# Attention with a rotary cache and a LoRA layer on one core: the query projection moved ahead of the third scores, the value products behind them, weight pieces taken three steps ahead

## The chip, the core and the metric

One core of one Trainium2 chip runs the whole program. The metric is the device time in microseconds (us) of one execution. TensorE (PE in the profile, with PEld for its weight loads), VectorE (DVE), ScalarE (ACT), GpSimd (POOL) and the queue of SyncE (SP) each work through their own list of instructions in order; one waits for another by semaphores.

## The reference

Two residual layers follow each other, x of 8 batches x 128 tokens x 512 features, all in float32:

```
q, k, v = x Wq^T (32 heads of 128), x Wk^T, x Wv^T (8 heads of 128 each)
q, k    = rope(rmsnorm(q) * wq), rope(rmsnorm(k) * wk)
keys    = [512 keys of the paged cache (masked from cache_seqlens on), 128 new keys]; values likewise
o       = softmax(q keys^T / sqrt(128) + mask) values, 4 query heads to a key head
x       = x + o Wo^T
x       = x + x W^T + 2 * sum_e gate[e] * (x A[e]^T) B[e]^T, gates from the top two of 8 experts
```

## The kernel before

The attention is cut into 64 groups, `g` = 0 to 63: eight key heads, the outer part, times eight batches. A group has four query heads (h = 0 to 3), 640 keys and 128 tokens. Every product on TensorE is made of float32r operands in three passes, `hi*hi + hi*lo + lo*hi`. So every operand is split into two tiles: ScalarE copies it to the high one (`..._hi`), and VectorE subtracts that from the original and writes the low one (`..._lo`, helper `low`, line 743).

The loop runs over steps `s` = 0 to 64, and each engine has its own `step(s)`, written out by hand; the order in that code is the order on the engine. The work of three groups is mixed in a step. With short names that the rest of this document uses, TensorE does in step s, before the change:

- S0, S1: scores of heads 0 and 1 of group s (`scores(h)`, line 1196), 6 products each, into `ps_s`
- V: value products of group s-1 (lines 289 to 291, out<-in `ps_w<-pt_..,v_..`), 15 products of 512 columns
- S2, then T0: scores of head 2; four transposes of the probabilities of head 0 (line 1205)
- Q: query projection of group s+2 (`project_queries`, `ps_w<-w_..,xt_..`), 12 products of 512 columns
- S3, T1, then Y: the output projection of group s-1 (`ps_w<-wo_..,o_..`), 12 products
- T2, QT and KTC (transposes of rotated queries and cached keys of group s+1), the key and value projection of group s+2 with KTN (new keys turned) in it, T3, and TN (line 1273), which ends the step

A head h of group s goes S, then on VectorE `rowmax(h)` (line 833, which adds the mask and takes the maximum), on ScalarE `exps(h)` (line 599), on VectorE the reciprocal `over_sum(h)` (line 840), on ScalarE `norm(h)` (line 605), then T. The value products end in `o_hi` (ScalarE) and then `o_lo` (VectorE), and Y waits for `o_lo` (`d_olo`).

The queries of group s+1 are normed and rotated in step s. ScalarE squares them, VectorE sums the squares (`sumsq`, line 799), GpSimd makes `meansq` (439), `rstd` (441, a power of five numbers) and `wr` (459), VectorE multiplies `u<-raw,wr` (879). Then two products of `u` start: `m<-u,sin` on VectorE (806, called m2 in the code) and `rot<-u,cos` on GpSimd (447), and GpSimd adds the two (465).

`ps_w` has four banks of PSUM, given out by rotation over the list `UNITS`; `wait_bank` makes TensorE wait until the unit that had the bank before was read. The weights of the next key head come in eight pieces (`W_AT` for q, k, v, `WO_AT` for Wo: step to pieces; `W_MID`, `WO_MID`: a second place in early steps). ScalarE splits a piece's high half in the step that the table names, VectorE its low half (`w_lo`, `wo_lo`) in the next, and the SP queue loads it in the step before. Steps 0 to 8 also hold work that is done once: masks, splits of x, the first Wo.

## Time and profile before

| what | value |
|---|---|
| time, median of 3 runs | 1173.83 us (1172.22 to 1174.01) |
| the profiled execution | 1173.76 us, span of its instructions 1172.0 us |
| TensorE busy | 1147.9 us, 98% |
| VectorE, ScalarE, GpSimd busy | 920.5, 934.3, 764.8 us |
| TensorE's mean granted clock | 0.998 of full speed |

The span reaches from the first to the last instruction. TensorE's products overlap, so their durations add up to more than the time between their starts; below, lengths on TensorE are differences of starts.

### The profile page before, as it was taken

The page shows a single profiled execution, that of the slowest core. Times are in us where ns is not written, and L with a number is a line of the kernel's source. Part 1 is how long each engine was busy: PE and PEld are TensorE (multiplying, and loading weights), DVE is VectorE, ACT ScalarE, POOL GpSimd, SP SyncE. Part 2 cuts the span into 40 slices and gives each one's busy share as a digit, 9 for nine tenths or more (in the row PEclk, how much of TensorE's full clock was granted, in tenths as well). Part 3 has the DMA queues.
Part 4 walks back from the last instruction along what each step waited for, and adds up shares of the span by engine and source line. Part 5 has one row for each costly group of instructions (what it writes and reads, how often), then busy time and mean ns, then how long its engine had stood idle before and what let it go on. Part 6 is the DMA issues. An engine that isn't in the chain of part 4 may idle for free.

```text
span 1172.0 us, 20839 instructions
## 1 busy us (share of the span) xinstructions
PE 1147.9 (98%) x6932; PEld 1025.8 (88%) x6932; DVE 920.5 (79%) x1885; ACT 934.3 (80%) x1832; POOL 764.8 (65%) x834
## 2 busy tenths in 40 slices
PE   6899999999999999999999999999999999999898
PEld 5788888889989988988998899899889989989787
DVE  7878788777887877788787778878777887877746
ACT  6788887888888888888888888888888888888741
POOL 4767666767666766776676676667667666766500
PEclk9999999999999999999999999999999999999999
DMA  6333332122123212312321221222122122211001
GB/s 242 130 96 108 105 100 89 54 95 95 61 83 96 89 54 95 95 53 90 95 87 57 95 95 56 88 95 86 58 95 95 52 89 93 83 48 61 19 1 72
DMA packets 53738, 98.11 MB, mean 84 GB/s; under 512 B 8704, under 2 KB 25984, under 8 KB 53376
## 3 DMA queue, kind: packets, MB, share of 16 engines
q1 hardware_dynamic: 41344, 63.21, 15.6%
q0 software_dynamic: 12288, 33.57, 9.5%
q8 instruction: 57, 0.93, 0.3%
q14 instruction: 49, 0.40, 0.1%
HBM read 90.45 MB, written 6.29 MB: 83 GB/s over the span
## 4 chain that ended last, share of the span: by engine, by line
PE 92%; DVE 3%; ACT 2%; issue 1%; DVEq 0%; ACTq 0%
PE ps_s L1196 18%; PE ps_w L289 18%; PE ps_w L291 18%; PE ps_w L290 18%; PE ps_w L1205 9%; PE ps_w L1273 3%; PE ps_w L1172 2%; PE ps_w L1179 2%; PE ps_s L1127 2%; DVE pt_lo L743 1%; ACT ps L599 1%; DVE ps L833 1%; PE ps_w L1150 1%; ACT ps L605 1%; DVE wo_lo L743 0%
## 5 line engine op out<-in xcount | busy, mean ns | idle before, releaser
L429 POOL DMA_INDIRECT kv_raw<-kv,rows x256 | 255.0, 996 | 97.0 <-issue 62.3
L599 ACT ACTIVATE ps<-ps,negmax 128x640 f32<-128x640 f32 x256 | 211.8, 827 | 91.0 <-DVE negmax L833 91.0
L605 ACT ACTIVATE ps<-ps,recip 128x640 f32<-128x640 f32 x256 | 213.0, 832 | 67.3 <-DVE recip L840 67.3
L743 DVE TENSOR_TENSOR pt_lo<-ps_w,pt_hi 128x512 fp32r<-128x512 f32 x322 | 209.9, 683 | 67.7 <-ACT pt_hi L610 66.5
L833 DVE CUSTOM_DVE_ANT_0 ps<-ps_s,mask 128x640 f32<-128x640 f32 x256 | 204.0, 815 | 2.2 <-PE ps_s L1196 1.2
L289 PE MATMUL ps_w<-w_hi,xt_hi 128*128 128x512 f32 (+1 forms) x496 | 182.5, 368 | 3.6 <-DVE w_lo L743 2.2
L610 ACT ACTIVATE pt_hi<-ps_w 128x512 fp32r<-128x512 f32 x256 | 151.8, 593 | 24.3 <-PE ps_w L1205 21.3
L447 POOL TENSOR_TENSOR rot<-u,cos 128x640 f32<-128x640 f32 x63 | 99.4, 1578 | 107.0 <-DVE u L879 107.0
L291 PE MATMUL ps_w<-w_hi,xt_lo 128*128 128x512 f32 (+1 forms) x496 | 167.4, 338 | 0.0
L290 PE MATMUL ps_w<-w_lo,xt_hi 128*128 128x512 f32 (+1 forms) x496 | 167.0, 337 | 0.0
L1205 PE MATMUL ps_w<-cst,ps 128*128 128x128 f32 x1024 | 154.1, 273 | 4.6 <-DVE pt_lo L743 2.2
L465 POOL TENSOR_TENSOR rot<-rot,m 128x320 f32<-128x320 f32 x126 | 108.7, 885 | 51.6 <-DVE m L806 51.5
L1205 PEld LDWEIGHTS ps_w<-cst,ps 128*128 128x128 f32 x1024 | 123.8, 141 | 16.0 <-issue 5.7
L290 PE MATMUL ps_w<-pt_lo,v_hi 128*128 128x512 f32 x320 | 125.4, 392 | 0.0
L289 PE MATMUL ps_w<-pt_hi,v_hi 128*128 128x512 f32 x320 | 125.3, 392 | 0.0
L1196 PE MATMUL ps_s<-kt_hi,qt_hi 128*128 128x320 f32 x512 | 122.2, 320 | 3.1 <-DVE kt_lo L743 2.8
L291 PE MATMUL ps_w<-pt_hi,v_lo 128*128 128x512 f32 x320 | 124.9, 390 | 0.0
L806 DVE TENSOR_TENSOR m<-u,sin 128x640 f32<-128x640 f32 x64 | 123.2, 1925 | 0.0
L1196 PE MATMUL ps_s<-kt_hi,qt_lo 128*128 128x320 f32 x512 | 117.4, 311 | 0.0
L840 DVE RECIPROCAL recip<-rowsum 128x1 f32<-128x1 f32 x256 | 41.0, 160 | 97.3 <-ACT ps L599 96.9
L1196 PE MATMUL ps_s<-kt_lo,qt_hi 128*128 128x320 f32 x512 | 117.1, 310 | 0.0
L289 PE MATMUL ps_w<-wo_hi,o_hi 128*128 128x512 f32 x256 | 105.6, 412 | 0.0
(172 smaller groups left out, 2642.1 us busy)
## 6 DMA issues: line engine op xcount, KB each, us to landing
xt_hi<-xsplit SPq DMA_DIRECT2D x56, 256.0 KB, 3.1
xt_lo<-xsplit SPq DMA_DIRECT2D x56, 256.0 KB, 3.7
w_raw<-wqkv SPq DMA_DIRECT2D x56, 192.0 KB, 3.8
wo_raw<-wo SPq DMA_DIRECT2D x56, 128.0 KB, 4.1
kv_raw<-kv,rows POOLq DMA_INDIRECT x256, 3.9
y<-x SPq DMA_DIRECT2D x8, 256.0 KB, 3.8
out<-y SPq DMA_DIRECT2D x8, 256.0 KB, 2.3
xsplit<-xt_hi SPq DMA_DIRECT2D x6, 256.0 KB, 3.3
```

What stands on the lines that cost most here:

```text
L289: nc.tensor.matmul(out_ap, a_hi, b_hi, start=start and k == 0, stop=False)
L290: nc.tensor.matmul(out_ap, a_hi, b_lo, start=False, stop=False)
L291: last = nc.tensor.matmul(out_ap, a_lo, b_hi, start=False, stop=stop and k == n - 1)
L429: pool.indirect_dma_start(kv_raw[:, g % 2, t, :], None, kv[:, :], bass.IndirectOffsetOnAxis(rows[:, g % B, t:t + 1], 0)).then_inc(s_kv[g % ...
L599: nc.scalar.activation(ps[:, h, :], ps[:, h, :], ACT.Exp, bias=negmax[:, s % 2, h:h + 1], scale=-1.0, accum_out=rowsum[:, s % 2, h:h + 1]) ...
L605: nc.scalar.activation(ps[:, h, :], ps[:, h, :], ACT.Copy, scale=recip[:, s % 2, h:h + 1]).then_inc(a_norm, 1)
L610: nc.scalar.activation(pt_hi[:, 0:CT, h, :], bank(f"T{h}").rearrange("p (t q) -> p t q", t=CT), ACT.Copy).then_inc(a_pt, 1)
L743: return nc.vector.tensor_tensor(out_ap, full, hi.bitcast(F32), ALU.subtract)
L806: nc.vector.tensor_tensor(m2[:], u[:], sin[:, g % B, :].unsqueeze(1).to_broadcast([P, NH, D]), ALU.mult).then_inc(d_m2, 1)
L833: nc.vector.tensor_tensor_reduce(out=halves(ps[:, h, :]), in0=ps_s[:, h % 2, :, 0:KH], in1=halves(mask[:, b, :]), scale=-SCALE, scalar=3.0 ...
L1196: last = nc.tensor.matmul(ps_s[:, h % 2, half, 0:KH], a, c[:, half * KH:(half + 1) * KH], start=n == 0, stop=n == 2)
L1205: last = nc.tensor.transpose(bank(f"T{h}")[:, t * S:(t + 1) * S], ps[:, h, t * P:(t + 1) * P], ident)
```

## The change

The order on three engines moves. On TensorE, Q stands behind S1 now, then S2, V and T0. On ScalarE the copy of the queries and exps(2), norm(2) stand ahead of `o_hi`. On VectorE the first piece of weights is taken behind the sum of squares instead of behind over_sum(1), and `o_lo` behind `m` instead of ahead of rowmax(2). The bank list is turned by one place to match. The tables `W_MID` and `WO_MID` are gone; pieces are split one step earlier. Masks, splits of x and the first Wo move to other places of steps 0 to 5. No instruction is added or removed in the steady steps.

```diff
@@ -68,7 +68,7 @@
...
-UNITS = ["O", "T0", "Q", "T1", "Y", "T2", "QT", "KTC", "KV", "KTN", "T3", "TN"]
+UNITS = ["Q", "O", "T0", "T1", "Y", "T2", "QT", "KTC", "KV", "KTN", "T3", "TN"]
 NU = len(UNITS)
@@ -79,12 +79,10 @@
...
 OP = REP * HID // B
-W_AT = {2: [2], 3: [4], 4: [6], 5: [7]}
-W_MID = {1: 0, 2: 1, 3: 3, 4: 5}
+W_AT = {1: [0, 1], 2: [2, 3], 3: [4, 5], 4: [6, 7]}
 for n in range(B, HK * B):
-    W_AT[n - 2] = [n]
-WO_AT = {3: [0], 4: [1], 5: [2], 6: [4], 7: [6], 8: [7]}
-WO_MID = {6: 3, 7: 5}
+    W_AT[n - 3] = [n]
+WO_AT = {5: [0, 1], 6: [2, 3], 7: [4, 5], 8: [6, 7]}
 for n in range(B, (HK - 1) * B + 2):
@@ -252,6 +250,12 @@
...
             return ps_w[:, UNITS.index(unit) % NBANK, :]
+
+        def query_bank(g):
+            return bank("T0") if g == 1 else bank("Q")
+
+        def keys_values_bank(g):
+            return bank("O") if g == 0 else bank("KV")
@@ -390,16 +394,12 @@
...
                     x_transposed(2, 1, 0, 4)
-                if s + 1 in W_MID:
-                    w_load(W_MID[s + 1])
                 for n in W_AT.get(s + 1, ()):
...
                     natural_x(1)
-                if s + 1 in WO_MID:
-                    wo_load(WO_MID[s + 1])
                 for n in WO_AT.get(s + 1, ()):
@@ -559,12 +559,12 @@
...
                 wait(act, d_u, g - 2)
-                nc.scalar.activation(raw[:, g % 2, 0:QW], bank("Q"), ACT.Copy).then_inc(a_q, 1)
+                nc.scalar.activation(raw[:, g % 2, 0:QW], query_bank(g), ACT.Copy).then_inc(a_q, 1)
...
                 wait(act, p_v, g - 2, 2)
-                nc.scalar.activation(raw[:, g % 2, QW:WW], bank("KV")[:, 0:2 * D], ACT.Copy).then_inc(a_kv, 1)
+                nc.scalar.activation(raw[:, g % 2, QW:WW], keys_values_bank(g)[:, 0:2 * D], ACT.Copy).then_inc(a_kv, 1)
@@ -617,6 +617,8 @@
...
                         first_wo_split(h)
+                if HB < s + 3 < B:
+                    split_x(s + 3)
                 if has(s):
@@ -624,6 +626,12 @@
...
                     expert_products(0)
+                if has(g2):
+                    queries(g2)
+                turn_x(s, "Q")
+                if has(s):
+                    exps(2)
+                    norm(2)
                 if has(s - 1):
@@ -641,25 +649,17 @@
...
                     nc.scalar.activation(v_hi[:, CT, :], raw[:, s % 2, QW + D:WW], ACT.Copy).then_inc(a_vhi, 1)
-                    if HB <= s + 3 < B:
-                        split_x(s + 3)
-                    exps(2)
-                    norm(2)
-                if has(g2):
-                    queries(g2)
-                turn_x(s, "Q")
                 if has(s):
                     probs(1)
-                    if s in W_MID:
-                        w_split(W_MID[s])
-                    if s in WO_MID:
-                        wo_split(WO_MID[s])
                     exps(3)
                     norm(3)
-                    probs(2)
                 if s == 0:
...
                         first_wo_split(h)
+                elif s == 1:
+                    split_x(HB)
+                if has(s):
+                    probs(2)
                 if has(g1):
@@ -850,18 +850,37 @@
...
                     sums_of_squares(g1)
+                if s == 0:
+                    split_x(3)
+                elif s == 1:
+                    first_wo_split(2)
+                for n in W_AT.get(s - 1, ())[:1]:
+                    w_split(n)
+                for n in WO_AT.get(s - 1, ())[:1]:
+                    wo_split(n)
                 if has(s):
...
                     add_base(0)
-                if s in (1, 2):
-                    masks(3 * s - 1, 3 * s + 1)
-                for n in W_AT.get(s - 1, ()):
+                if s == 1:
+                    first_wo_split(3)
+                for n in W_AT.get(s - 1, ())[1:]:
                     w_split(n)
-                for n in WO_AT.get(s - 1, ()):
+                for n in WO_AT.get(s - 1, ())[1:]:
                     wo_split(n)
+                if has(s):
+                    rowmax(2)
+                if has(g1):
+                    wait(dve, p_wr, g1 - 1)
+                    wait(dve, d_ss, g1)
+                    nc.vector.tensor_tensor(u[:].rearrange("p h d -> p (h d)"), raw[:, g1 % 2, 0:QW + D],
+                                            wr[:].rearrange("p h d -> p (h d)"), ALU.mult).then_inc(d_u, 1)
+                if has(s):
+                    over_sum(2)
+                if has(g1):
+                    times_sine(g1)
                 if has(s - 1):
@@ -870,53 +889,35 @@
...
                 if has(s):
-                    rowmax(2)
-                if s == 0:
-                    split_x(3)
-                if has(g1):
-                    wait(dve, p_wr, g1 - 1)
-                    wait(dve, d_ss, g1)
-                    nc.vector.tensor_tensor(u[:].rearrange("p h d -> p (h d)"), raw[:, g1 % 2, 0:QW + D],
-                                            wr[:].rearrange("p h d -> p (h d)"), ALU.mult).then_inc(d_u, 1)
-                if has(s):
-                    over_sum(2)
-                if has(g1):
-                    times_sine(g1)
-                if has(s):
                     rowmax(3)
...
                     over_sum(3)
+                if HB <= s + 3 < B:
+                    split_x(s + 3)
+                elif s == 0:
+                    first_wo_split(0)
+                if 0 <= s < HB + 1:
+                    masks(s + 2, s + 3)
                 if 0 < s <= B:
...
                     nc.vector.tensor_tensor(yb, bank("Y"), yb, ALU.add).then_inc(d_y, 1)
-                if HB <= s + 3 < B:
-                    split_x(s + 3)
-                if s == 0:
-                    first_wo_split(0)
-                    first_wo_split(1)
                 if has(s):
                     probs(2)
-                if s == 0:
-                    first_wo_split(2)
                 if has(g1):
...
                 if s == 0:
-                    first_wo_split(3)
-                if s in W_MID:
-                    w_split(W_MID[s])
-                if s in WO_MID:
-                    wo_split(WO_MID[s])
+                    first_wo_split(1)
                 if has(g1):
                     new_keys(g1)
-                if s in (1, 2):
-                    masks(3 * s + 1, 3 * s + 2)
+                if s == HB:
+                    masks(B - 1, B)
                 for unit in ("QT", "KTC", "KV", "KTN"):
@@ -1135,22 +1136,29 @@
...
                         pe.wait_ge(d_wlo, SPLITS + g)
-                wait_bank(pe, g - 2, "Q")
+                if g >= 2:
+                    wait_bank(pe, g - 2, "Q")
...
                 wh, wl = head_weights(g // B)
-                three_passes(bank("Q"), [(xt_tile(0, g, k), xt_tile(1, g, k), wh[:, k, 0:QW], wl[:, k, 0:QW])
+                three_passes(query_bank(g), [(xt_tile(0, g, k), xt_tile(1, g, k), wh[:, k, 0:QW], wl[:, k, 0:QW])
                                          for k in range(KC)], before=weights_split).then_inc(pe_q, 1)
...
             def turn_new_keys(g):
-                wait_bank(pe, g - 1, "KTN")
+                if g == 0:
+                    wait(pe, a_kv, 0)
+                else:
+                    wait_bank(pe, g - 1, "KTN")
                 nc.tensor.transpose(bank("KTN")[:, 0:S], rot[:, REP, :], ident).then_inc(pe_ktn, 1)
...
             def project_keys_values(g, new_keys_of=None):
-                wait_bank(pe, g - 2, "KV")
+                if g == 1:
+                    wait(pe, a_q, 0)
+                elif g >= 2:
+                    wait_bank(pe, g - 2, "KV")
@@ -1159,15 +1167,17 @@
...
                 wh, wl = head_weights(g // B)
-                three_passes(bank("KV")[:, 0:2 * D], [(xt_tile(0, g, k), xt_tile(1, g, k), wh[:, k, QW:WW], wl[:, k, QW:WW])
+                three_passes(keys_values_bank(g)[:, 0:2 * D], [(xt_tile(0, g, k), xt_tile(1, g, k), wh[:, k, QW:WW], wl[:, k, QW:WW])
                                                       for k in range(KC)], before=between).then_inc(pe_kv, 1)
...
                     pe.wait_ge(d_scaled, NH - 2)
-                wait(pe, p_rot, g - 1, 2)
-                wait_bank(pe, g - 1, "QT")
+                    wait(pe, a_q, 1)
+                else:
+                    wait(pe, p_rot, g - 1, 2)
+                    wait_bank(pe, g - 1, "QT")
                 for h in range(REP):
@@ -1210,29 +1220,25 @@
...
                     second_layer(0)
+                if has(g2):
+                    project_queries(g2)
+                turn_x(s, "Q")
+                if has(s):
+                    scores(2)
                 if has(s - 1):
-                    wait(pe, d_pt, s - 1, 5, CT)
+                    wait(pe, d_pt, s - 1, 5)
                     wait(pe, p_v, s - 1, 2)
                     wait_bank(pe, s, "O")
-
-                    def new_keys_split(t):
-                        if t == CT:
-                            wait(pe, d_pt, s - 1, 5)
-
                     three_passes(bank("O"), [(v_hi[:, t, :], v_lo[:, t, :],
                                               pt_hi[:, t, :, :].rearrange("p h q -> p (h q)"),
-                                              pt_lo[:, t, :, :].rearrange("p h q -> p (h q)")) for t in range(KT)],
-                                 before=new_keys_split).then_inc(pe_o, 1)
+                                              pt_lo[:, t, :, :].rearrange("p h q -> p (h q)")) for t in range(KT)]
+                                 ).then_inc(pe_o, 1)
                 if s == G:
...
                 if has(s):
-                    scores(2)
                     turn_probs(0)
-                if has(g2):
-                    project_queries(g2)
-                turn_x(s, "Q")
                 if has(s):
...
                     turn_probs(1)
```

TensorE, the stretch that ends with the first product of Y, a steady step, before (first row: last product of Q; L1196 is S3, L1205 is T1):

```order
L291 MATMUL ps_w<-w_hi,xt_lo 128x512
L1196 MATMUL ps_s<-kt_hi,qt_hi 128x320 x2
L1196 MATMUL ps_s<-kt_lo,qt_hi 128x320 x2
L1196 MATMUL ps_s<-kt_hi,qt_lo 128x320 x2
L1205 MATMUL ps_w<-cst,ps 128x128 x4
L289 MATMUL ps_w<-wo_hi,o_hi 128x512
```

The same stretch of the change (first row: last product of V; then T0, S3, T1):

```order
L295 MATMUL ps_w<-pt_hi,v_lo 128x512
L1215 MATMUL ps_w<-cst,ps 128x128 x4
L1206 MATMUL ps_s<-kt_hi,qt_hi 128x320 x2
L1206 MATMUL ps_s<-kt_lo,qt_hi 128x320 x2
L1206 MATMUL ps_s<-kt_hi,qt_lo 128x320 x2
L1215 MATMUL ps_w<-cst,ps 128x128 x4
L293 MATMUL ps_w<-wo_hi,o_hi 128x512
```

The last value product now stands two transposes and one head's scores ahead of Y; before, Q and S2 stood between as well.

VectorE in the same step, from over_sum(0) to `m`, before (RECIPROCAL is over_sum, ISA the two halves of rowmax):

```order
L840 RECIPROCAL recip<-rowsum 128x1
L799 TENSOR_REDUCE sumsq<-u 128x5
L840 RECIPROCAL recip<-rowsum 128x1
L743 TENSOR_TENSOR w_lo<-w_raw,w_hi 128x384
L743 TENSOR_TENSOR wo_lo<-wo_raw,wo_hi 128x256
L743 TENSOR_TENSOR o_lo<-ps_w,o_hi 128x512
L833 ISA ps,negmax<-ps_s,mask 128x640
L833 ISA negmax 128x1
L879 TENSOR_TENSOR u<-raw,wr 128x640
L840 RECIPROCAL recip<-rowsum 128x1
L806 TENSOR_TENSOR m<-u,sin 128x640
```

And in the change, to `o_lo`:

```order
L840 RECIPROCAL recip<-rowsum 128x1
L799 TENSOR_REDUCE sumsq<-u 128x5
L743 TENSOR_TENSOR w_lo<-w_raw,w_hi 128x384
L743 TENSOR_TENSOR wo_lo<-wo_raw,wo_hi 128x256
L840 RECIPROCAL recip<-rowsum 128x1
L833 ISA ps,negmax<-ps_s,mask 128x640
L833 ISA negmax 128x1
L878 TENSOR_TENSOR u<-raw,wr 128x640
L840 RECIPROCAL recip<-rowsum 128x1
L806 TENSOR_TENSOR m<-u,sin 128x640
L743 TENSOR_TENSOR o_lo<-ps_w,o_hi 128x512
```

The low halves of the weights moved ahead of over_sum(1), and `o_lo` moved behind five rows, the long `m` among them.

ScalarE in the same step, from the second exps to `o_hi`, in the change (L599 exps, L605 norm, L562 the copy of the queries); before, `o_hi` stood right behind the first norm here:

```order
L599 ACTIVATE ps,rowsum<-ps,negmax 128x640
L605 ACTIVATE ps<-ps,recip 128x640
L562 ACTIVATE raw<-ps_w 128x512
L599 ACTIVATE ps,rowsum<-ps,negmax 128x640
L605 ACTIVATE ps<-ps,recip 128x640
L638 ACTIVATE o_hi<-ps_w 128x512
```

So `o_hi` now waits, by its place in the queue, for norm(2), and norm(2) for the third reciprocal on VectorE, which stands behind `u`.

## Rows read from the trace of the kernel before

**Rows 1.** Windows view, all engines: length; busy and (instructions) by engine; clock; DMA

```profile
41.00:60.00 19.00, 18.96 (x104) 16.95 (x104) 13.81 (x30) 13.93 (x28) 13.02 (x14) 0.91 0.41 143
590.00:607.00 17.00, 17.00 (x105) 15.34 (x104) 13.53 (x27) 14.13 (x29) 12.10 (x14) 1.00 0.25 82
```

**Rows 2.** Chain that ended last, S0 with S1 of a step: start, us, what

```profile
41.04 3.48 PE ps_s L1196 x12
...
113.78 2.00 PE ps_s L1196 x12
...
218.20 1.75 PE ps_s L1196 x12
...
1073.49 1.76 PE ps_s L1196 x12
```

**Rows 3.** Timeline of TensorE, one steady step: start, us, instruction

```profile
611.48 0.54 PE L1196 MATMUL ps_s<-kt_hi,qt_hi 128*128 128x320 f32 x2
...
620.82 0.45 PE L1196 MATMUL ps_s<-kt_hi,qt_hi 128*128 128x320 f32 x2
...
622.05 0.48 PE L289 MATMUL ps_w<-wo_hi,o_hi 128*128 128x512 f32 x1
```

**Rows 4.** Timeline of VectorE, the same step

```profile
614.97 0.82 DVE L799 TENSOR_REDUCE sumsq<-u 128x5 f32<-128x640 f32 x1
...
616.84 0.54 DVE L743 TENSOR_TENSOR w_lo<-w_raw,w_hi 128x384 fp32r<-128x384 f32 x1
617.30 0.42 DVE L743 TENSOR_TENSOR wo_lo<-wo_raw,wo_hi 128x256 fp32r<-128x256 f32 x1
618.31 0.69 DVE L743 TENSOR_TENSOR o_lo<-ps_w,o_hi 128x512 fp32r<-128x512 f32 x1 [0.59 <-ACT o_hi L630]
...
619.65 0.82 DVE L879 TENSOR_TENSOR u<-raw,wr 128x640 f32<-128x640 f32 x1
...
620.81 1.99 DVE L806 TENSOR_TENSOR m<-u,sin 128x640 f32<-128x640 f32 x1
```

**Rows 5.** Timeline of ScalarE, the same step

```profile
616.96 0.83 ACT L605 ACTIVATE ps<-ps,recip 128x640 f32<-128x640 f32 x1 [0.23 <-DVE recip L840]
617.70 0.57 ACT L630 ACTIVATE o_hi<-ps_w 128x512 fp32r<-128x512 f32 x1
```

**Rows 6.** Timeline of GpSimd, the same step

```profile
615.88 0.20 POOL L439 TENSOR_SCALAR meansq<-sumsq 128x5 f32<-128x5 f32 x1 [0.95 <-DVE sumsq L799]
...
617.45 1.39 POOL L459 TENSOR_TENSOR wr<-nw,rstd 128x640 f32<-128x640 f32 x1
```

**Rows 7.** Timeline of all engines, ahead of the first step

```profile
17.86 0.82 DVE L806 TENSOR_TENSOR m<-u,sin 128x640 f32<-128x640 f32 x1
...
18.11 0.62 POOL L439 TENSOR_SCALAR meansq<-sumsq 128x5 f32<-128x5 f32 x1 [2.77 <-DVE sumsq L799]
...
18.59 0.82 DVE L992 TENSOR_TENSOR rot<-u,cos 128x640 f32<-128x640 f32 x1
...
18.82 1.66 POOL L441 TENSOR_TENSOR rstd<-meansq,mhalf 128x5 f32<-128x5 f32 x1
```

**Rows 8.** Timeline of all engines, step 0: the pair of `m` and `rot`

```profile
29.45 1.26 POOL L459 TENSOR_TENSOR wr<-nw,rstd 128x640 f32<-128x640 f32 x1
...
31.18 0.81 DVE L879 TENSOR_TENSOR u<-raw,wr 128x640 f32<-128x640 f32 x1
...
31.91 0.15 DVE L840 RECIPROCAL recip<-rowsum 128x1 f32<-128x1 f32 x1
32.02 0.82 DVE L806 TENSOR_TENSOR m<-u,sin 128x640 f32<-128x640 f32 x1
...
32.07 2.22 POOL L447 TENSOR_TENSOR rot<-u,cos 128x640 f32<-128x640 f32 x1 [1.36 <-DVE u L879]
```

**Rows 9.** The same view, step 0: T0 behind the norm that releases it

```profile
27.04 0.83 ACT L605 ACTIVATE ps<-ps,recip 128x640 f32<-128x640 f32 x1 [0.23 <-DVE recip L840]
...
27.92 0.66 PE L1205 MATMUL ps_w<-cst,ps 128*128 128x128 f32 x4 [0.86 <-ACT ps L605]
```

14 lines of the change are left out of this document (7 added, 7 removed).

## The prediction

> **What bounds the kernel now.** I read the windows view first. In a steady stretch of 17 us TensorE is busy for all of it, VectorE and ScalarE for about 14 us each [rows 1]. So TensorE is the bound, and a change can only give back what TensorE idles, or add to it. Next the chain of waits, which shows where each step begins (S0 and S1 stand as one piece of 12 products). From 218.20 to 1073.49 lie 50 steps: 17.106 us each [rows 2]. The early steps are longer. Steps 1 to 4 take 113.78 - 41.04 = 72.74 us, 4.32 above four steady ones; steps 5 to 10 take 104.42, 1.78 above six steady ones [rows 2]. Of the 4.32, S0 and S1 of step 1 account for 3.48 - 1.75 = 1.73 us [rows 2]: there the granted clock fell, to a mean of 0.91 over 19 us against 1.00 later [rows 1]. By the two levels, 1.2 and 2.4 GHz, that is about 3.4 us at the lower one, after a step 0 in which TensorE often stood still. What is left, 2.6 us in steps 1 to 4, is TensorE waiting at the step's start for VectorE.
>
> The rest of the argument is one steady step, the one that starts at 611.48, and I count from there. Y starts at 10.57 [rows 3]. In the trace o_lo is done at 618.31 + 0.69, which is 7.52 [rows 4], so Y has 3 us to spare. `u` starts at 8.17 and `m` at 9.33.
>
> **What costs nothing.** The steady step holds the same products in another order. Between V and Y now stand T0, S3 and T1. S3 with T1 takes 622.05 - 620.82 = 1.23 us [rows 3], T0 at most 0.44 (estimated from T1's part of it), so V ends at about 8.9 and its last result leaves the array near 9.1. Y stays at 10.57 if nothing holds it. Q at the place of V needs the bank that V needed before, so it waits for the same copy. V waits for all of its operands at once now, but starts later by Q and S2. Moving weight pieces one step earlier puts their loads one step earlier in SP's queue, ahead of the x loads that stand behind them; each of those has a step or more before its use, so I take nothing. The cover is a whole step; without it each late load would stop Q.
>
> **The new chain to Y.** It has three parts.
>
> First, the way to `u`. The sum of squares starts at 3.49 and VectorE is free for the next instruction after about 0.73 us, as `m` and the next product show [rows 7]. There now stands `w_lo`: 4.22 to 4.76. `wo_lo` follows after 617.30 - 616.84 = 0.46 and lasts 0.42 [rows 4]: 4.68 to 5.10. GpSimd starts `meansq` at 4.40, where it took 0.20 [rows 6]. Ahead of step 0 the trace shows what happens when VectorE works on two SBUF tiles then: `meansq` took 0.62 and ended at 18.73, 0.05 after `m` ended, although the next VectorE product had begun at 18.59; the `rstd` behind it started 0.09 later, took 1.66 and ended at 20.48, 1.07 after that second product [rows 7]. So GpSimd is held while such an instruction runs, and gets in between two of them. Applied here: `meansq` ends at 4.81, `rstd` at 5.10 + 1.07 = 6.17, `wr` starts 0.09 later, 6.26. `wr` took 1.39 behind a `wo_lo` that still ran as it began [rows 4, 6]; nothing does now, and without that it takes 1.26 [rows 8]. It ends at 7.52, and with 0.05 for the handover (T0 started at 27.92, the norm ended at 27.87 [rows 9]) `u` runs from 7.57 to 8.39. In the trace it starts at 8.17.
>
> Second, `m`. It takes 1.99 in the steady step [rows 4], but 0.82 in step 0 [rows 8]. In step 0 the reciprocal was ready, `m` started 0.84 after `u` and GpSimd's `rot` 0.89 after it; `m` ran through and `rot` took 2.22 [rows 8]. In the steady step the reciprocal comes late, `rot` goes first and `m` is held until `rot` is done. In the new order exps(2) stands ahead of V's copy. Norm(1) starts at 5.48 [rows 5], the copy of the queries 0.74 later, exps(2) some 0.5 behind that and takes about 0.9 with its sum, estimated from the norm's 0.83: it ends near 7.65, well before `u` does. So the case of step 0 comes in every step: `m` from 8.41 to 9.23. VectorE gets back 1.17 us a step, which by itself is worth nothing on the path.
>
> Third, the copies. The third reciprocal starts at 7.57 + 0.73 = 8.30 and lasts 0.15 [rows 8]; with 0.05 for the handover norm(2) starts on ScalarE at 8.50. `o_hi` follows a norm after 617.70 - 616.96 = 0.74 [rows 5]: 9.24, later than V's end. `o_lo` follows after 618.31 - 617.70 = 0.61 [rows 4, 5]: 9.85, and lasts 0.69: 10.54. With 0.05 to reach TensorE Y starts at 10.59, 0.02 later than it would, or a little more if the weight load ahead of its first product has to be waited for too. Each of these seven handovers is good to 0.01 or 0.02, so the bounds are nothing and 0.13 a step. I choose 0.08, above the walk, because an early result gives nothing back while each late one adds its delay. Behind Y on TensorE are T2, the turned queries and keys, and T3, and ScalarE and VectorE follow them, so the wait lengthens each step and is not caught up. There are 61 such steps (1 to 61): 4.9 us.
>
> The Trainium skill bears on the first part. "SBUF — State Buffer", section "Who interferes with whom", says that a VectorE instruction with two SBUF inputs and a GpSimd instruction that reads SBUF exclude each other for a whole instruction; the trace agrees with its 0.62 for 0.20 [rows 7]. The same page, in its section on the bandwidth-pool intuition, states a release about 115 ns after VectorE ends where the row shows 0.05. By the page `meansq` would end 0.065 later, and 61 steps differ by 4 us. The sum goes by the row.
>
> **What is given back.** In steps 2 to 4 low halves of weights stood ahead of the new keys on VectorE, and S0 of the next step waits for those. They are gone from there. In their place ScalarE now has two high pieces ahead of its new-key copy in steps 1 to 4. A piece is of the size of `w_lo`, 0.54 [rows 4], and most of it fits into the time in which ScalarE waits for the new keys; I take 0.15 us a step (bounds 0 and 0.54). So of 2.6 us 2.0 come back (bounds 0.4 and 2.6). The 1.78 us of steps 5 to 10 I did not break down; the change has fewer pieces in their middle, and I take 0.4 (bounds 0 and 1.78). In step 0 Q runs while TensorE waited for norm(0), 0.86 us [rows 9]; the step ends on VectorE's and GpSimd's work, and I take 0.6 (bounds 0 and 1.2). Together 3.0. The last two steps have no Q; Y comes later there, and `m` is shorter: nothing, within 0.7 either way.
>
> **Sum.** 1173.76 of the profiled execution, less 3.0, plus 4.9: 1175.7. The median, 1173.83, is the same within 0.1.
>
> **The rivals.**
> - A, the forecast: a wait of 0.03 to 0.13 at Y. The sum reaches from 1172.0 to 1179.5. Chance 0.60.
> - B, no wait at Y: GpSimd isn't held by `w_lo`, `u` starts at about 7.3 and `o_lo` is done by 10.4. For it: in the steady trace `w_lo` runs at 616.84, between `meansq` at 615.88 and `wr` at 617.45, and did not stretch that distance of 1.57 visibly [rows 4, 6]. Against it: rows 7. Only the 3.0 us remain: 1169.5 to 1171.5. Chance 0.15.
> - C, ends on the slow side by far: `rot` keeps its lead over `m`. The lead that decides is 0.05 us, in one pair of rows [rows 8]. If the reciprocal or the wait on `u` makes `m` start more than 0.05 later, `m` ends 622.80 - 619.65 = 3.15 after `u` starts, as in the trace [rows 4]: 10.72, `o_lo` at 11.33, Y at 11.4. That is 0.82 x 61 = 50 us, less 3.0: 1221. Against it: the same start in step 0, with the reciprocal ready. Chance 0.07.
> - D, a larger wait of the same kind, 0.15 to 0.4 a step: `meansq` has to wait for `wo_lo` as well, since that one is queued before `w_lo` ends (then `u` starts 0.28 later). Rows 7 speak against it. 9 to 24 us less 3.0: 1180 to 1195. Chance 0.14.
> - E, 0.04: step 0 leaves TensorE busy enough that the clock does not fall in step 1, and the 1.7 us come back on top of A: about 1174.
>
> **How the numbers follow.** The measurement tells 0.2%, 2.3 us, from no change. Case A splits into 0.05 faster, 0.31 the same, 0.24 slower. B gives 0.13 faster and 0.02 the same, C and D 0.21 slower, E 0.02 faster and 0.02 the same. Together 0.20, 0.35, 0.45. The range takes in A, nearly all of B and the lower third of D: 1169.5 to 1183. A's own is 1172 to 1179.5.
>
> **What the new profile would show.** `m` at 0.82 and `rot` at 2.2 in all steps: second part right; `m` at 2.0: case C. `meansq` at about 0.4, with `w_lo` beside it: first part right; at 0.20: case B; at 0.75: D. `u` 7.57 after S0, `o_lo` ending at 10.5. A mean step of 17.19 between the S0 of steps 11 and 61; 17.11 is B, 17.3 and more is D. Steps 1 to 4 at about 70.7 us without the wait at Y. I would be wrong by several microseconds if one of the handovers on the way from `u` to Y is off by 0.1 us, since 61 steps multiply it; and wrong in sign if ScalarE takes `o_hi` earlier than its place in the queue suggests, which nothing in the order allows.

## The result: 0.8% slower, and where the profile puts it

| | before | after |
|---|---|---|
| median of the runs shown together | 1173.92 us | 1184.06 us (1182.77 to 1185.02, 4 runs) |
| ratio | | 1.0083, interval 1.0071 to 1.0095 |
| span of the profiled execution | 1172.0 us | 1181.0 us |

Two further groups of runs of the same kernel, on other chips, gave 1183.46 and 1184.68, ratios 1.0071 and 1.0086. The forecast was 1175.7 with a range up to 1183: the direction was right, the size was not.

The windows view of the changed kernel, read as [rows 1], now with a third window near the end:

```profile
41.00:60.00 19.00, 18.14 (x106) 16.19 (x106) 14.15 (x29) 14.79 (x29) 13.79 (x16) 0.95 0.37 123
590.00:607.00 17.00, 17.00 (x105) 15.23 (x104) 12.46 (x28) 13.83 (x29) 12.55 (x14) 1.00 0.26 82
...
1093.00:1128.00 35.00, 27.60 (x150) 23.41 (x149) 20.32 (x45) 24.27 (x47) 12.26 (x13) 0.90 0.05 15
```

The steady stretch looks as before, with VectorE 1.07 us freer. In the third window TensorE is busy for 27.60 of 35 us, at a mean clock of 0.90; before, the same stretch reads 31.02 at 1.00, though its steps lie 3 to 9 us earlier and part of it is already behind step 63. The waits view of TensorE (what it waited for: us in total, times, longest) names what stands there:

```profile
PE ps_w L293 <- DVE w_lo L743: 8.0, 6, 3.5
...
PE ps_w L293 <- DVE y L909: 2.9, 4, 0.9
PE ps_w L1182 <- POOL rot L465: 2.4, 1, 2.4
...
PE ps_w L293 <- DVE o_lo L743: 0.9, 1, 0.9
```

A wait at Y in each steady step isn't in this view at all: each is too short to be listed. It has to be read from the chain, whose S0 with S1 of steps 11 and 61 now stand here (as [rows 2]):

```profile
218.22 1.76 PE ps_s L1206 x12
...
1076.47 1.76 PE ps_s L1206 x12
```

That is 858.25 / 50 = 17.165 us a step, against 17.106. For the two last steps I went by TN, the last thing of a step on TensorE. First the timeline of the changed kernel, then that of the kernel before:

```profile
1092.90 0.60 PE L1279 MATMUL ps_w<-cst,ps 128*128 128x128 f32 x4
...
1114.25 0.65 PE L1279 MATMUL ps_w<-cst,ps 128*128 128x128 f32 x4
...
1132.66 0.66 PE L1279 MATMUL ps_w<-cst,ps 128*128 128x128 f32 x4
```

```profile
1089.96 0.66 PE L1273 MATMUL ps_w<-cst,ps 128*128 128x128 f32 x4
...
1107.64 0.66 PE L1273 MATMUL ps_w<-cst,ps 128*128 128x128 f32 x4
...
1123.64 0.66 PE L1273 MATMUL ps_w<-cst,ps 128*128 128x128 f32 x4
```

Step 62 went from 17.68 to 21.35 us, step 63 from 16.00 to 18.41. The difference of the two spans, each step from TN to TN, in us:

| steps | difference | what is seen there |
|---|---|---|
| up to 1 | -0.1 | |
| 2 to 4 | +0.7 | KV waits for `y` |
| 5 to 9 | -0.7 | |
| 10 to 53 | +3.3 | the wait at Y |
| 54 to 61 | -0.3 | |
| 62 and 63 | +6.1 | Y waits 3.53 and 3.15 for `w_lo` |
| all | +9.0 | |

The part up to TN of step 0 can't be compared so finely: it lasted 39.84, 42.63 and 40.83 us in the three traces of the changed kernel (this one, c1 and c3 below), and 39.98 before. The other rows are steps, and c1 and c3 show them alike.

**The ending.** In steps 62 and 63 there is no Q; in its place TensorE turns a piece of x into bank 0 (`TURN_X`), ScalarE writes its high half, VectorE its low half (`final_x(c)[1]`, in the profile `w_lo<-ps_w,w_hi`). Timeline of VectorE in step 62 of the changed kernel, and below it TensorE's last transposes ahead of Y and Y's products with `o_hi`:

```profile
1102.88 0.69 DVE L743 TENSOR_TENSOR o_lo<-ps_w,o_hi 128x512 fp32r<-128x512 f32 x1 [0.59 <-ACT o_hi L638]
1103.48 0.81 DVE L833 CUSTOM_DVE_ANT_0 ps<-ps_s,mask 128x640 f32<-128x640 f32 x1
...
1104.22 0.69 DVE L743 TENSOR_TENSOR pt_lo<-ps_w,pt_hi 128x512 fp32r<-128x512 f32 x1
1104.83 0.68 DVE L743 TENSOR_TENSOR w_lo<-ps_w,w_hi 128x512 fp32r<-128x512 f32 x1
```

```profile
1101.53 0.60 PE L1215 MATMUL ps_w<-cst,ps 128*128 128x128 f32 x4
1105.65 0.77 PE L293 MATMUL ps_w<-wo_hi,o_hi 128*128 128x512 f32 x1 [3.53 <-DVE w_lo L743]
...
1107.07 0.63 PE L293 MATMUL ps_w<-wo_hi,o_hi 128*128 128x512 f32 x1
...
1108.35 0.63 PE L293 MATMUL ps_w<-wo_hi,o_hi 128*128 128x512 f32 x1
```

T1 starts at 1101.53, and Y could follow it at about 1101.9. `o_lo` is done at 1103.57. But the new `UNITS` puts Y behind Q in bank 0, and the turned x in Q's place leaves that bank only when its low half is written, at 1105.51; that instruction still stands behind the fourth row maximum and the first low half of the probabilities, where it stood when Q itself came late. So Y waits for an instruction that needs nothing from the row maximum and only stands behind it. The granted clock fell to the lower level during the wait: Y's groups of three products are 1.28 us apart (1107.07 to 1108.35), against 0.69 at full clock, 2.4 us over the four. The windows view of Y in this step has the clock:

```profile
1105.65:1110.91 5.26, 5.25 (x12) 4.00 (x13) 0.53 (x2) 0.83 (x1) 1.45 (x2) 0.50 0.00 0
```

In step 63 Y waited 3.15 us and ran at the full clock. The sum of the two steps closes: 6.7 us of waits at Y and 2.4 by the clock came in; in the kernel before, TensorE waited 1.57, 1.42 and 0.85 us for low halves of probabilities in these steps, and of such waits 0.54 and 0.20 are left. That makes 6.0 of the 6.1 us.

**A steady step.** Timelines of the changed kernel in the step whose S0 starts at 613.05, VectorE, then GpSimd, ScalarE and TensorE (compare [rows 3 to 6]):

```profile
616.63 0.82 DVE L799 TENSOR_REDUCE sumsq<-u 128x5 f32<-128x640 f32 x1
617.36 0.55 DVE L743 TENSOR_TENSOR w_lo<-w_raw,w_hi 128x384 fp32r<-128x384 f32 x1
617.83 0.42 DVE L743 TENSOR_TENSOR wo_lo<-wo_raw,wo_hi 128x256 fp32r<-128x256 f32 x1
...
620.69 0.83 DVE L878 TENSOR_TENSOR u<-raw,wr 128x640 f32<-128x640 f32 x1 [1.14 <-POOL wr L459]
...
621.55 0.83 DVE L806 TENSOR_TENSOR m<-u,sin 128x640 f32<-128x640 f32 x1
622.97 0.69 DVE L743 TENSOR_TENSOR o_lo<-ps_w,o_hi 128x512 fp32r<-128x512 f32 x1 [0.59 <-ACT o_hi L638]
```

```profile
617.54 0.44 POOL L439 TENSOR_SCALAR meansq<-sumsq 128x5 f32<-128x5 f32 x1 [1.77 <-DVE sumsq L799]
...
621.59 2.21 POOL L447 TENSOR_TENSOR rot<-u,cos 128x640 f32<-128x640 f32 x1 [0.94 <-DVE u L878]
```

```profile
621.62 0.83 ACT L605 ACTIVATE ps<-ps,recip 128x640 f32<-128x640 f32 x1 [0.88 <-DVE recip L840]
622.36 0.58 ACT L638 ACTIVATE o_hi<-ps_w 128x512 fp32r<-128x512 f32 x1
```

```profile
623.27 0.60 PE L1215 MATMUL ps_w<-cst,ps 128*128 128x128 f32 x4
623.71 0.50 PE L293 MATMUL ps_w<-wo_hi,o_hi 128*128 128x512 f32 x1
```

`meansq` lasts 0.44 and ends 0.07 after `w_lo`; `u` starts 7.64 after S0, `m` lasts 0.83 and starts 0.04 ahead of `rot`, `o_lo` ends at 10.61, Y starts at 10.66. Y starts 0.44 after T1, where it would start 0.36 after it if nothing held it (below, e10): a wait of 0.08 to 0.09 us.

### The profile page after: what moved, and what is told of

The parts are those of the page before. It is cut to its first block, busy times and chain, and to the rows that moved or that the text cites. A ratio compares the mean times of both kernels' runs of the same rounds, so it can differ in the third digit from the quotient of the medians.

```text
span 1181.0 us, 20838 instructions
## 1 busy us (share of the span) xinstructions
PE 1152.6 (98%) x6932; PEld 1028.8 (87%) x6932; DVE 860.7 (73%) x1885; ACT 917.4 (78%) x1832; POOL 813.8 (69%) x834
## 4 chain that ended last, share of the span: by engine, by line
PE 88%; DVE 4%; issue 2%; ACT 2%; POOL 2%; DMA 1%; SPq 0%; DVEq 0%; POOLq 0%; ACTq 0%
PE ps_w L293 18%; PE ps_w L295 17%; PE ps_w L294 17%; PE ps_s L1206 17%; PE ps_w L1215 9%; PE ps_w L1279 2%; PE ps_w L1189 2%; PE ps_w L1182 2%; PE ps_s L1128 2%; DVE pt_lo L743 1%; ACT ps L599 1%; DVE ps L833 1%; POOL wr L459 1%; POOL rstd L441 1%; PE ps_w L1155 1%
## 5 line engine op out<-in xcount | busy, mean ns | idle before, releaser
L605 ACT ACTIVATE ps<-ps,recip 128x640 f32<-128x640 f32 x256 | 213.0, 832 | 102.1 <-DVE recip L840 102.1
L599 ACT ACTIVATE ps<-ps,negmax 128x640 f32<-128x640 f32 x256 | 211.3, 825 | 37.9 <-DVE negmax L833 37.7
L293 PE MATMUL ps_w<-w_hi,xt_hi 128*128 128x512 f32 (+1 forms) x496 | 177.3, 357 | 4.1 <-DVE y L909 2.1
L447 POOL TENSOR_TENSOR rot<-u,cos 128x640 f32<-128x640 f32 x63 | 139.2, 2210 | 59.1 <-DVE u L878 59.1
L1206 PE MATMUL ps_s<-kt_hi,qt_hi 128*128 128x320 f32 x512 | 127.7, 331 | 1.8 <-DVE kt_lo L743 1.6
L293 PE MATMUL ps_w<-wo_hi,o_hi 128*128 128x512 f32 x256 | 108.1, 422 | 7.6 <-DVE w_lo L743 6.7
L439 POOL TENSOR_SCALAR meansq<-sumsq 128x5 f32<-128x5 f32 x64 | 27.4, 428 | 114.4 <-DVE sumsq L799 112.5
L293 PEld LDWEIGHTS ps_w<-w_hi,xt_hi 128*128 128x128 f32 x496 | 93.4, 188 | 14.3 <-DVE y L909 2.8
```

The costliest lines, as they stand in the source:

```text
L293: nc.tensor.matmul(out_ap, a_hi, b_hi, start=start and k == 0, stop=False)
L447: nc.gpsimd.tensor_tensor(rot[:].rearrange("p h (t d) -> p (h t) d", t=2), u[:].rearrange("p h (t d) -> p (h t) d", t=2), cos[:, g % B, :] ...
L599: nc.scalar.activation(ps[:, h, :], ps[:, h, :], ACT.Exp, bias=negmax[:, s % 2, h:h + 1], scale=-1.0, accum_out=rowsum[:, s % 2, h:h + 1]) ...
L605: nc.scalar.activation(ps[:, h, :], ps[:, h, :], ACT.Copy, scale=recip[:, s % 2, h:h + 1]).then_inc(a_norm, 1)
L1206: last = nc.tensor.matmul(ps_s[:, h % 2, half, 0:KH], a, c[:, half * KH:(half + 1) * KH], start=n == 0, stop=n == 2)
```

## The experiments

Eighteen runs, in five groups; each group ran on one chip, beside the kernel before. In two of the groups, e1 to e4 and e11 to e13, something came in that no other trace shows: semaphore increments late or missing ("disturbed" below). Their times answer nothing; single rows of them do. The last section has what they show.

### The ending alone: e1, and again e8

```diff
                 if has(g1):
                     times_sine(g1)
+                turn_x(s, "Q")
                 if has(s - 1):
                     wait(dve, a_o, s - 1)
@@ the same call, behind rowmax(3) and probs(0), is taken out
```

> The changed kernel with one edit: VectorE writes the low half of the turned x in bank 0 (steps 62 and 63) ahead of the low half of the attention output, no longer behind the third probabilities' row maximum and the first low half of the probabilities. Theory (bank 0 is given back late, because its last reader stands behind work that waits for the transposes and the fourth scores): the two waits of Y on w_lo, 3.53 and 3.15 us, go, step 62 falls from 21.35 to about 17.7 us and step 63 from 18.41 to about 16.0; 4.8 to 6.1 us in all, so 1178 to 1179.3. Rival (the granted clock falls there for a reason of its own and its spell stretches Y by about 2.4 us whatever w_lo does): the waits go, but products at the lower clock stay in step 62 and the time falls by no more than 4.3 us, to 1179.8 or above.

Measured: 1226.34, ratio 1.0432 (1.0417 to 1.0446), in a disturbed group. The waits at Y in steps 62 and 63 had gone, as both theories wanted, but 0.9 us had come in nearly every steady step.

> e1_turned_x once more, unchanged. In its first trace the semaphore increments themselves come late or not at all (of 8,576 increments by transfers the trace holds 5,546, against 8,570 to 8,576 in the kernels without the wait; the increment of the second scores stands 1.3 us after its place). Theory 1 (something disturbed the group of runs in which e1 to e4 stood, not the kernel): 1177 to 1180, all increments in the trace and no wait of 1.2 us at the row maximum. Theory 2 (the order of instructions in e1 brings the late increments about): about 1226 again, increments missing again.

Measured: 1176.3, ratio 1.0025 (1.0012 to 1.0038), 0.7 below theory 1's range, with the increments in the trace: theory 1. Steps 62 and 63 lasted 16.80 and 16.43 us. The windows view of e8, same stretch as above:

```profile
1093.00:1128.00 35.00, 31.46 (x195) 27.08 (x193) 24.06 (x53) 27.91 (x54) 12.60 (x13) 1.00 0.05 16
```

The clock is 1.00 here and no idle 3.5 us are left, so in the profiled execution e1's rival (a fall for its own reason) is out. Three of the ten runs took 1179.3 to 1181.2 at a mean granted clock of 0.992 to 0.995, against 0.995 to 0.997 in the others; no trace shows where it fell in those. By the ratios, 1.0083 and 1.0025, one moved call took 6.8 us off, and 6.5 are seen in the two steps. It is not all that could be had there: Y still waits 1.49 and 1.13 us for `o_lo`.

### The control, and the later gathers: c1, e5, e6, c2

> The changed kernel without any edit, on the chip that runs the next ones, since three of the four edits brought some 45 us that neither theory had: in each steady step of those, the second row maximum on VectorE starts 1.2 us late, 0.93 us after the end of the fourth gather instruction (DMA_INDIRECT) on GpSimd, while the changed kernel's rows show the same two instructions at the same places without that wait. Theory 1 (the wait comes from the edited orders, in some way that is still to be found): 1184 again, no wait at the row maximum. Theory 2 (the changed kernel stands at the edge of that wait, and which side it falls on differs from chip to chip or run to run): about 1225, with a wait of 1.2 us in some 50 steps.

Measured: 1183.46, ratio 1.0071 (1.0056 to 1.0087); no wait at the row maximum.

```diff
                         gather(s + 2)
+                        wait(pool, a_ktc, s + 1)
                         gather_dma(s + 2)
```

> e1_turned_x with one more edit: GpSimd starts the gathers of step s+2 only once ScalarE has copied the cached keys of step s+1, so that the four gather instructions start at -1.0, 0.4, 1.7 and 2.9 us from TN, as in the kernel before, and not at -1.8, -0.4, 0.9 and 2.1. Theory (a gather instruction that is running as VectorE hands over from the first row maximum to the second, 2.78 us after TN, takes the memory port until 0.93 us after its own end; 2.1 to 3.1 hits the handover, 1.7 to 2.6 and 2.9 to 3.9 miss it): the wait of 1.2 us goes, steady steps are 17.1 to 17.2 us again and the two waits of Y on w_lo are gone as well, 1177 to 1180. Rival (where the gathers stand does not matter and the wait comes with the order of VectorE's instructions): the wait stays and the time is within 2 us of 1226.

Measured: 1178.94, ratio 1.0039 (1.0026 to 1.0053), no such wait. This looked like my theory and is not evidence for it, since this group was not disturbed and e8, in another quiet group, has the same ending without the later gathers at 1176.3.

> The kernel before with one edit: GpSimd starts the gathers of step s+2 only when TensorE has turned the new keys of step s+1, some 0.4 us later than now, so that the third gather instruction runs from about 2.1 to 3.1 us after TN, over VectorE's handover between the first two row maxima at 2.78 us. Theory (a gather instruction under the handover holds the second row maximum until 0.93 us after its end): the second row maximum starts at 3.9 to 4.0 us after TN in nearly all steps and the kernel is 0.3 to 0.9 us a step slower, 1190 to 1225. Rival (the wait belongs to the changed order on VectorE alone): no wait at the row maximum and 1174 to 1176.

The edit is the same line with `pe_ktn`, in the kernel before. Measured: 1173.8, ratio 0.9998 (0.9989 to 1.0008). The third gather now ran from about 2.3 to 3.3 us after TN, across the handover at 2.78, in nearly every step, and the second row maximum started on time. That refutes the theory as it stood, that a gather over the handover is enough. This group was quiet, so whether the place of the gathers matters in a disturbed one isn't shown.

> The changed kernel with the later gathers of e5 alone, as the base for the next two. In the changed kernel nothing waits for the gathers or at their place, so 1183 to 1185 if they cost nothing; 1182 or less, or 1186 or more, would mean that e5 and e7 owe a part to them.

Measured: 1182.61, ratio 1.0070 (1.0054 to 1.0085). By the ratios that is 0.0001 to 0.0016 below the changed kernel's three groups, while e5 is 0.0014 above e8: within 2 us either way, and no clear sign.

### `o_hi` ahead of the second normalisation: e3, and with the later gathers e10

```diff
                     exps(2)
-                    norm(2)
                 if has(s - 1):
                     wait(act, pe_o, s - 1)
                     wait(act, pe_y, s - 2)
                     nc.scalar.activation(o_hi[:], bank("O"), ACT.Copy).then_inc(a_o, 1)
+                if has(s):
+                    norm(2)
```

> The changed kernel with one edit: on ScalarE the high half of the attention output (o_hi) stands ahead of the normalisation of head 2, in place of behind it. Theory (Y waits 0.07 to 0.085 us a step, because o_hi waits for its turn behind the normalisation, which itself waits for u on VectorE): o_hi starts as V ends, about 0.3 us earlier, o_lo with it, the wait at Y goes and a steady step falls from 17.18 to about 17.10 us; 3.3 to 4.4 us in some 52 steps, 1179.7 to 1180.8. Rival (the chain through the normalisation of head 2 is as tight as that through o_lo, so the normalisation that is now about 0.5 us later makes the third transposes or what follows wait): a wait at the third transposes takes its place and the time stays at 1183.5 to 1185.

Measured: 1184.2, ratio 1.0075 (1.0059 to 1.0090), disturbed; steps without a late increment were 17.05 long, the others up to 17.6.

> The later gathers and e3's edit: the high half of the attention output ahead of the normalisation of head 2 on ScalarE. Theory (its place in that queue is what makes Y wait in each steady step): o_lo ends 0.2 to 0.3 us earlier, steady steps 17.05 in place of 17.17 us, 6 to 7 us less than c2, about 1177. Rival (in e7 it was another of the edits that took the 0.12 us a step): steady steps stay at 17.17 and the time within 1 us of c2.

Measured: 1173.79, ratio 1.0001 (0.9992 to 1.0010): 8.8 us less than c2, more than I expected. Timelines of e10, ScalarE and TensorE, in the step whose S0 starts at 609.21:

```profile
618.30 0.60 ACT L638 ACTIVATE o_hi<-ps_w 128x512 fp32r<-128x512 f32 x1 [1.41 <-PE ps_w L295]
618.80 0.82 ACT L606 ACTIVATE ps<-ps,recip 128x640 f32<-128x640 f32 x1
```

```profile
619.42 0.60 PE L1217 MATMUL ps_w<-cst,ps 128*128 128x128 f32 x4
619.78 0.48 PE L293 MATMUL ps_w<-wo_hi,o_hi 128*128 128x512 f32 x1
```

`o_hi` now waits for V itself and starts at 9.09, not at 9.31. Y starts 0.36 after T1, and every steady step is 17.05 to 17.06 us. This is below the 17.10 of the kernel before. Over steps 11 to 53 S0 starts 0.39 after TN there and 0.36 here, and TN 0.46 after T3 there and 0.44 here. The changed kernel without any edit has the same 0.36 and 0.44. So the new order is by itself worth 0.05 us a step, and the late `o_hi` took 0.12 in the changed kernel, not 0.06 to 0.07; the chain showed only the net. The ending changed too: steps 62 and 63 together came down from 39.96 us in c2 to 37.09, since `w_lo` stands behind an earlier `o_lo` (step 62 from 21.52 to 18.11; step 63 rose from 18.44 to 18.98, because Y ran partly at the lower clock there).

### The place of `w_lo`: e4, again e11; e12, again e14

e4 puts `w_lo` and `wo_lo` behind `rowmax(2)`, where VectorE waits 1.14 us for `wr`; e12 puts `w_lo` alone ahead of the addition to `y`:

```diff
                     over_sum(3)
+                if s > B + 1:
+                    for n in W_AT.get(s - 1, ()):
+                        w_split(n)
@@ and not behind sums_of_squares from step 10 on
```

> The changed kernel with one edit: from step 10 on, the low halves of the weight pieces (w_lo, wo_lo) stand on VectorE behind the third row maximum, in the 1.14 us in which it waits for wr, and no longer between sumsq and the second reciprocal. Theory 1 (meansq on GpSimd lasts 0.44 in place of 0.20 and starts late because w_lo and wo_lo hold the memory port that the two engines share; there the pair would now stand beside wr, and one of them has to give way): meansq falls to 0.20 and rstd and wr start 0.3 to 0.4 us earlier, but u starts no earlier than 7.5 us after S0, since wr is stretched or the pair ends only behind it; the time stays within 1.5 us of 1184.1, or rises by up to 5 us if the pair is held until wr ends and u stands behind it. Theory 2 (only the order in VectorE's queue counts and nothing is shared): u starts 0.3 us or more earlier, the wait at Y goes, 1179.7 to 1180.8.

> e4_w_lo once more, unchanged, since its first run stood in the disturbed group. There w_lo lasted 1.47 us beside wr in place of 0.55, wo_lo and u stood behind it, and the steps without a late increment were 17.59 and 17.52 us long. Theory 1 (one memory port for the two engines, which the later one has to wait for): again w_lo of 1.4 to 1.5 us, u 7.9 to 8.0 us after S0 although meansq is back to 0.20, steady steps of 17.55 to 17.6, so 0.4 us in 53 steps more than the changed kernel, 1202 to 1207. Theory 2 (only the order counts): u no later than 7.4, 1180 or less.

Both runs fell into disturbed groups: e4 1250.14 and e11 1244.28, ratios 1.0637 (1.0624 to 1.0651) and 1.0599 (1.0583 to 1.0615). But the two engines' rows are plain. Timeline of e11, VectorE and GpSimd:

```profile
614.35 1.48 DVE L743 TENSOR_TENSOR w_lo<-w_raw,w_hi 128x384 fp32r<-128x384 f32 x1
```

```profile
612.58 0.20 POOL L439 TENSOR_SCALAR meansq<-sumsq 128x5 f32<-128x5 f32 x1 [2.52 <-DVE sumsq L799]
...
614.15 1.26 POOL L459 TENSOR_TENSOR wr<-nw,rstd 128x640 f32<-128x640 f32 x1
```

`meansq` is back at 0.20 with nothing beside it, and now `w_lo` lasts 1.48 in place of 0.55: it ends 0.42 after `wr`. Theory 1 of both. By the Trainium skill, "SBUF — State Buffer", section "Who interferes with whom", the one that comes second waits for the whole instruction of the other; the trace agrees, in both directions now. The two steps of each that no late increment touched were 17.52 to 17.59 long, 0.4 more than in the changed kernel; what that makes of the whole time in a quiet group was not measured.

> The changed kernel with one edit: from step 10 on, w_lo stands on VectorE ahead of the addition to y, where that engine waits 1.1 us for the output projection; wo_lo stays behind sumsq. Theory (the pair behind sumsq keeps meansq waiting until w_lo is written; with wo_lo alone there, which lasts 0.42 in place of 0.55 us, meansq ends 0.1 to 0.2 us earlier, and with it wr, u, the second normalisation, o_hi and o_lo): meansq 0.30 to 0.35, u about 7.5 us after S0, the wait at Y gone and steady steps of 17.10 us: 3 to 4 us less, 1180 to 1181. Rival (o_lo is set by o_hi's place behind the normalisation and not by meansq): steady steps stay at 17.17, 1183 to 1185.

> e12_w_lo_late once more, unchanged. In e12 the steps that no late increment touched were 17.13 us long, against 17.17 in the changed kernel, so in a group without late increments: 2 us less than the changed kernel, 1181 to 1182.5, u 7.5 to 7.6 us after S0 and a wait at Y of 0.03 to 0.05 us a step. That would give w_lo's place about half of the steady steps' loss and o_hi's place behind the normalisation the rest. With late increments: 1200 to 1210 again and no answer.

Measured: e12 1205.02, ratio 1.0269 (1.0246 to 1.0292), disturbed; e14 1181.34, ratio 1.0053 (1.0040 to 1.0067), 3.3 us less than the changed kernel in the same group (c3, below), of which the traces show 1.6 in steps 10 to 53. GpSimd and VectorE in e14, step with S0 at 615.23:

```profile
619.71 0.30 POOL L439 TENSOR_SCALAR meansq<-sumsq 128x5 f32<-128x5 f32 x1 [1.60 <-DVE sumsq L799]
```

```profile
622.67 0.83 DVE L879 TENSOR_TENSOR u<-raw,wr 128x640 f32<-128x640 f32 x1 [0.95 <-POOL wr L459]
...
627.66 1.60 DVE L743 TENSOR_TENSOR w_lo<-w_raw,w_hi 128x384 fp32r<-128x384 f32 x1
629.18 0.68 DVE L913 TENSOR_TENSOR y<-ps_w,y 128x512 f32<-128x512 f32 x1
```

TensorE in the same step, where the key and value projection (KV) begins:

```profile
629.51 0.60 PE L1193 MATMUL ps_w<-cst,kv_raw 128*128 128x128 f32 x4
629.92 0.38 PE L293 MATMUL ps_w<-w_hi,xt_hi 128*128 128x256 f32 x1
```

`u` starts at 7.44, 0.20 earlier, and Y starts 0.36 after T1: the wait at Y is gone, over steps 11 to 53 as in e10. Steady steps are 17.13 all the same, because the edit made a new wait. `w_lo`, beside GpSimd's low half of the values (1.30, from 627.55 on), lasts 1.60 in its new place, the addition to `y` ends at 629.86, and KV, which needs the bank that this frees, starts 0.41 after KTC in place of 0.36; with KTN that is 0.08 a step. So my expectation, that `w_lo` makes half of the wait at Y and the place of `o_hi` the other half, was wrong. The cause that the prediction named, `meansq` held by `w_lo`, makes the whole wait, and the place of `o_hi` behind the normalisation hands it on: either edit removes it. The changed kernel shows the same by itself: from step 54 on its `w_lo` has 324 columns and lasts 0.49, `meansq` lasts 0.38, Y starts 0.38 after T1, and the steps are 17.08 (17.10 in c1 and c3).

### The addition to `y`: e2, and with the later gathers e9

On VectorE `split_x(s + 3)` and `masks(s + 2, s + 3)` go behind the addition to `y`.

> The changed kernel with one edit: on VectorE the addition to y stands ahead of split_x and of the mask in steps 1 to 4, in place of behind them. Theory (KV waits in those steps for y alone, which is late by the two instructions put ahead of it): the waits of TensorE at KV on y, 0.86, 0.67, 0.71 and 0.71 us, go and nothing takes their place, 2.3 to 2.9 us less, 1181.2 to 1181.8. Rival (the low half of the third probabilities, now behind the same two instructions, frees its bank late and turning the new keys waits in turn): the waits change their place, and the time stays within 1 us of 1184.1.

> The later gathers and e2's edit: the addition to y ahead of split_x and of the mask. Theory: the waits of TensorE at KV on y in steps 1 to 4 (0.9, 0.7, 0.7, 0.7 us) go for about half, since e7's steps 2 to 4 were 17.69 us long against 18.06 in the changed kernel: 1.2 to 2.9 us less than c2. Rival (the two instructions put behind y make the third probabilities and the new keys late for as much): within 0.5 us of c2.

Measured: e2 1229.02, ratio 1.0458 (1.0444 to 1.0473), disturbed. e9 1183.21, ratio 1.0075 (1.0061 to 1.0089), not below c2's 1182.61. The waits on `y` are gone and steps 2 to 4 are 17.69 in place of 18.06 us, 1.1 in all, less than I had hoped: counted from the start of KV, turning the new keys starts 0.3 later than in a steady step, and T3 0.2 more. In the same trace steps 62 and 63 were 0.4 longer than c2's. The two medians do not tell 1 us apart.

### Together: e7, e13, and again c3 and e15

> e1_turned_x, e2_y_first, e3_o_hi and the later gathers of e5 in one kernel. If the terms add up: the ending gives back 4.8 to 6.1 us, the early steps 2.3 to 2.9, o_hi ahead of the second normalisation 0.08 to 0.13 us in some 52 steps (3.3 to 6.6; e3's steps without a wait at the row maximum were 17.05 us long, against 17.18 in the changed kernel), so 1184.1 less 10.4 to 15.6, 1168.5 to 1173.7, below the kernel before. Rival (any of the three waits gives its time to the next one, or the row maximum still meets a gather in part of the steps): 1175 or more.

Measured: 1167.3, ratio 0.9945 (0.9932 to 0.9959), 1.2 below the expected range. The terms add up. The span fell by 15.7 us, from 1181.0 to 1165.3: 7.5 in steps 62 and 63, 6.8 in steps 5 to 61, 1.1 in steps 2 to 4 and 0.3 ahead of them; single edits gave 6.5 (e8), 7.3 (e10 against c2) and 1.1 (e9) there. In e7 steady steps are 17.05, and steps 62 and 63 are 16.72 and 15.55 us. Its waits view:

```profile
PE ps_w L1183 <- POOL rot L465: 2.4, 1, 2.4
PE ps_w L293 <- DVE o_lo L745: 1.9, 3, 1.4
...
PE ps_w L293 <- DVE w_lo L745: 1.5, 3, 0.7
```

> e1's and e3's edits alone: the low half of the turned x ahead of o_lo, and o_hi ahead of the normalisation of head 2. If the later gathers are worth nothing and the addition to y ahead of split_x 1.1 us in steps 2 to 4, this is 1 to 2 us above e7's 1167.3: 1167.5 to 1169.5, still 0.995 to 0.996 of the kernel before. Rival (the gathers at their earlier places are near some edge, as the first runs of e1 to e4 seemed to say): steps with a wait at the row maximum, 1172 or more.

Measured: 1177.58, ratio 1.0033 (1.0022 to 1.0044), disturbed, no answer on the gathers.

> The changed kernel without any edit. If this group shows no late increments: 1181 to 1185, as twice before. If it shows them: theory 1 (any kernel with the changed order is hit, since its gathers, its weight loads and its first two row maxima fall together) about 1225, steady steps of 18.0; theory 2 (only edited versions are hit) 1184.

Measured: 1184.68, ratio 1.0086 (1.0070 to 1.0101), no late increments in this group.

> e7_all once more, unchanged. Without late increments 1166.5 to 1169. With them: if the later gathers keep it clear of them as the order of the kernel before does, 1167 to 1170 as well; if they do not, 0.3 to 0.9 us in a steady step more, 1180 to 1215.

Measured: 1169.23, ratio 0.9943 (0.9929 to 0.9958). So the order of the change is 0.55% faster than the kernel before with four edits. Two of them, the turned x on VectorE and `o_hi` on ScalarE, make most of it; c2 and e9 show little for the other two. The two alone were run only in a disturbed group (e13), so their time is not measured; there the steps that no late increment touched are 17.05 and the last two 16.75 and 15.56, as in e7.

## Why the prediction was wrong, step by step

- **The step that failed** is the sentence on the ending: "The last two steps have no Q; Y comes later there, and `m` is shorter: nothing, within 0.7 either way." It was +6.1 us, and e8 takes it away. I had checked for Q which bank it needs, but not for Y which unit stands ahead of it in the new `UNITS`, nor who frees that bank in steps where Q is replaced. Of 64 steps, two with another content cost twice what the other 62 did.
- **The steady wait at Y** was right in mechanism, place and size. Forecast and measured: `meansq` about 0.4 and 0.44; `u` 7.57 and 7.64; `o_lo` 10.54 and 10.61; step 17.19 and 17.165. e14 takes away the first link, e10 the last, and the wait at Y goes each time. That the step came out as forecast is partly luck: I took the new order of products as worth nothing, it is worth 0.05 a step, and the loss by the late `o_lo` is larger by that, 0.12 in place of 0.08. My term, 61 steps of 0.08, was 4.9; steps 10 to 61 brought 3.0.
- **`m` and `rot`** traded places in all 63 steps as forecast (0.83 and 2.21), and the lead was 0.04 or 0.05 throughout. Case C did not come.
- **The early steps** failed too, by less. From TN of step 0 to TN of step 4 it took 73.7 us, 0.8 more than before, where I had 2.0 less. What should leave the start of the step did leave it: in steps 2 to 4 S0 starts 0.36 after TN, in place of 0.87. But I took the move of `split_x` and the masks as free; they went ahead of the addition to `y`, and KV waited 0.86, 0.67, 0.71 and 0.71 for that. e9 shows that even without this wait only 1.1 us come back.
- **Steps 5 to 10** gave about 0.6 for the 0.4 forecast. What step 0 gave (0.6 forecast) can't be told from the 0.1 between two traces, since the part up to its TN differs by up to 2.8 us from run to run.
- **Case E** did not come. The clock fell in step 1 by less, a mean of 0.95 over 41 to 60 us against 0.91, and S0 with S1 took 2.67 us against 3.48; but step 1 then waited 0.86 for `y` and lasted 19.54 against 19.44.
- **The range** ended at 1183 by case D, a larger wait in each step. No rival was about steps that differ from the rest. Without the wait on the turned x the kernel is e8, 1176.3, for the 1175.7 forecast, but that is luck in part, since two errors cancel: of the 3.0 us to be given back up to step 10 next to nothing came on balance, and steps 10 to 61 lost 3.0 where I had 4.9 for 1 to 61.

## What to carry to other kernels

When units rotate through banks, write down for each unit which one holds its bank ahead of it and which instruction frees it, in the last steps as well as in the steady one, and look where that instruction stands in its engine's queue. An instruction that only frees something should stand where its operands are ready, not behind one that waits. A wait of 0.1 us in every step is too short for the list of waits; the chain over 50 steps and the distance from one unit to the next show it.
